# Router logits formed in the attention stage instead of in the experts stage

## The reference

```python
x = x + tanh(g_xattn) * attention(layernorm(x), ctx, mask)      # 4 heads of 128, one key/value head, rope, softmax over 64
z = layernorm(x)                                                # the attention output x1, normed
logits = einsum('bntd,des->bntes', z.reshape(b, 32, 32, 512), Wc) + bc + tie     # 32 experts x 4 sets = 128 columns
perm = (logits == logits.max(axis=-3, keepdims=True))           # in each group of 32 tokens one token a column
picked = einsum('bntd,bntes->bnesd', z, perm)
inner = relu(picked @ W1 + b1)                                  # 32 wide, per expert and set
result = inner @ W2 + b2
x = x + tanh(g_ffn) * einsum('bnesd,bntes->bntd', result, perm)
```

## Time and profile before

| what | value |
|---|---|
| time, median of 3 runs | 1773.8 us (1768.51 to 1779.29) |
| the profiled execution's own time | 1778.45 us |
| its span, first to last instruction | 1776.7 us |
| mean granted TensorE clock | 0.987 of full speed |
| transfers | 325.90 MB, mean 183 GB/s |

### The profile page before, as it was taken

One profiled execution on the slowest core, in us unless ns is written; L12 is line 12 of the kernel. 1 busy time (PEld: TensorE's weight loads), 2 busy tenths in 40 slices (PEclk: granted clock), 3 DMA queues, 4 the chain that ended last, 5 costly groups with the idle time before them and its releaser, 6 DMA issues.

```text
span 1776.7 us, 53886 instructions
## 1 busy us (share of the span) xinstructions
PE 1663.9 (94%) x23384; PEld 1184.5 (67%) x23384; DVE 1335.7 (75%) x1974; ACT 822.0 (46%) x1073; POOL 623.2 (35%) x847
## 2 busy tenths in 40 slices
PE   7899999999999999979999999999999999999985
PEld 4677777777777777776576567657656765765662
DVE  6777777777777777737788778778877877787776
ACT  3433333333333333445555555565555556555542
POOL 3577777777777777410110011011011101100101
PEclk9999999999999999989999999999999999999997
DMA  7345454545555545353675575576457556645754
GB/s 263 130 144 167 144 173 151 178 151 183 159 167 155 168 144 176 120 187 104 227 238 156 197 247 178 184 236 234 155 200 249 177 194 227 241 150 201 247 180 155
DMA packets 161450, 325.90 MB, mean 183 GB/s; under 512 B 17344, under 2 KB 23232, under 8 KB 155840
## 3 DMA queue, kind: packets, MB, share of 16 engines
q1 hardware_dynamic: 156608, 288.91, 49.9%
q10 hardware_dynamic: 4608, 33.56, 4.8%
HBM read 254.25 MB, written 68.16 MB: 181 GB/s over the span
## 4 chain that ended last, share of the span: by engine, by line
PE 57%; DVE 15%; POOL 10%; issue 9%; ACT 5%; DMA 2%; SPq 0%; DVEq 0%; POOLq 0%; ACTq 0%
PE ps L1309 13%; PE ps L1282 8%; PE ps L1336 8%; PE ps L214 6%; PE ps L844 6%; PE ps L1351 4%; POOL qc L486 4%; POOL qc L487 4%; PE ps L200 4%; PE ps L1331 3%; DVE mx L612 2%; DVE qs L629 2%; PE ps L807 2%; DVE qc L628 2%; PE ps L787 2%
## 5 line engine op out<-in xcount | busy, mean ns | idle before, releaser
L182 POOL TENSOR_TENSOR b_va<-b_mv,eps_layer 128x2 f32<-128x2 f32 x64 | 12.5, 196 | 833.6 <-DVE b_mv L173 832.7
L1194 DVE STREAM_TRANSPOSE res<-res 128x2048 f32<-128x2048 f32 x128 | 292.0, 2295 | 0.1
L1146 ACT ACTIVATE gat<-ps 128x1536 f32<-128x1536 f32 (+1 forms) x128 | 172.2, 1345 | 198.2 <-PE ps L1282 198.2
L787 PE MATMUL ps<-xTh,qh 128*128 128x512 f32 x512 | 208.6, 407 | 7.0 <-DVE qs L629 5.4
L787 PE MATMUL ps<-xTl,qh 128*128 128x512 f32 x512 | 200.2, 391 | 0.0
L787 PE MATMUL ps<-xTh,ql 128*128 128x512 f32 x512 | 199.8, 390 | 0.0
L1216 DVE COPY res<-ps 128x1024 f32<-128x1024 f32 x128 | 156.7, 1224 | 43.7 <-PE ps L1336 43.7
L1282 PE MATMUL ps<-sel,xin 32*128 32x128 f32 x4096 | 153.7, 283 | 27.9 <-ACT sel L242 13.5
L1156 ACT ACTIVATE res<-ps 128x1024 f32<-128x1024 f32 x128 | 131.2, 1025 | 92.8 <-PE ps L1336 92.8
L1282 PEld LDWEIGHTS ps<-sel,xin 32*128 32x128 f32 x4096 | 129.4, 186 | 63.0 <-ACT gat L1146 40.1
L475 POOL TENSOR_TENSOR xTl<-xT,xTh 128x512 fp32r<-128x512 f32 x128 | 160.7, 1286 | 10.9 <-ACT xTh L522 10.9
(11 more groups left out here) (132 smaller groups left out, 3217.1 us busy)
## 6 DMA issues: line engine op xcount, KB each, us to landing
xin<-x_scratch SPq DMA_DIRECT2D x196, 256.0 KB, 4.0
xT<-in_xT SPq DMA_DIRECT2D x32, 1024.0 KB, 5.9
xin<-in_x SPq DMA_DIRECT2D x64, 512.0 KB, 3.8
x_scratch<-xin SPq DMA_DIRECT2D x64, 512.0 KB, 3.1
xin<-in_W SPq DMA_DIRECT2D x128, 256.0 KB, 3.5
gat<-in_W ACTq DMA_DIRECT2D x32, 1024.0 KB, 8.5
xT<-in_W SPq DMA_DIRECT2D x68, 256.0 KB, 4.0
gat<-in_W SPq DMA_DIRECT2D x64, 256.0 KB, 3.8
```

The source lines that it names most:

```text
L787: last = e.matmul(ps[:, 2 + n % 2, :], a[:, c, n * DH:(n + 1) * DH], b[:, c, :], start=(k == 0), stop=(k == len(parts) - 1))
L1146: e.activation(o, v, ACT.Copy).then_inc(m_gaA.sem, 1)
L1194: e.transpose(v, v).then_inc(m_tr.sem, 1)
```

## The change

The logits are linear in x1 up to the layer norm's factor and mean, and x1 is x plus probabilities times values times output weights. So the router weights are centred once (their mean over the width is taken off), and the logits before scaling are the sum of two products made in the attention stage: x by the centred weights (`part_of_x`, 12 fp32r matmuls a unit, before the probabilities are transposed), and the probabilities by `values * output weights * centred router weights` (`part_of_values`, 6 fp32r matmuls a unit, before `values`). The weights for the second are made in the set-up. ACT copies the first part, DVE adds the second (`both_parts`), and SP stores the 512 columns of a unit to `lg_scratch`. DVE also takes the statistics of x1 there, POOL makes the layer norm's factors (`row_scale`), and these are stored to `r_scratch`. The experts stage loads logits and factors by halves (`load_logits`), POOL multiplies them (`scaled`) and norms the x tiles (`normed`, formerly ACT), and DVE picks. Both halves use one place in SBUF, so the second load waits for the first pick. `turn`, `across`, `logits`, `stats` and `scale` are gone; the evictions of `outer` are divided 10 to 6 between ACT and DVE, the picks stand between DVE's evictions, the banks of `outer` are swapped, and the second of ACT's W2 loads stands behind the first eviction.

```diff
+W2_BY_ACT = ((0, 0), (1, 0), (2, 0), (2, 1), (3, 0), (4, 0), (5, 0), (5, 1), (6, 0), (7, 0))
+W2_BY_DVE = ((0, 1), (1, 1), (3, 1), (4, 1), (6, 1), (7, 1))
...
+    vc_dram = nc.dram_tensor("vc_scratch", (B, P, 2 * E), F32, kind="Internal").ap()
+    lg_dram = nc.dram_tensor("lg_scratch", (B, 2, E, HT), F32, kind="Internal").ap()
+    r_dram = nc.dram_tensor("r_scratch", (B, 2, P, TH), F32, kind="Internal").ap()
...
-    def stats(self, e, i, k):
-        for t in (2 * k, 2 * k + 1):
-            e.wait_ge(self.d_x[t].sem, self.d_x[t].at(i))
...
-    def scale(self, e, i, k):
...
+    def load_logits(self, e, i, h):
+        if h:
+            e.wait_ge(self.m_eq.sem, self.m_eq.at(i, 0))
+        v = self.room(i)
+        e.dma_start(v[:, 0:HT], self.lg_dram[i, h]).then_inc(self.d_lg.sem, 16)
+        e.dma_start(v[:, HT:2 * HT], self.r_dram[i, h].rearrange("p t -> (p t)").partition_broadcast(P)).then_inc(self.d_lg.sem, 16)
...
     def normed(self, e, i, t):
...
+        e.wait_ge(self.d_x[t].sem, self.d_x[t].at(i))
+        e.wait_ge(self.m_r.sem, self.m_r.at(i, t // TH))
+        e.tensor_scalar(self.xn[:, t, :], self.xn[:, t, :], self.r[:, i, t:t + 1], self.nb[:, i, t:t + 1],
+                        ALU.mult, ALU.add).then_inc(self.m_xn.sem, 1)
...
+    def scaled(self, e, i, h):
+        e.wait_ge(self.d_lg.sem, self.d_lg.at(i, 2 * h + 1))
+        v = self.room(i)
+        o = v[:, 0:HT].rearrange("p (t s) -> p t s", s=P)
+        e.tensor_tensor(o, o, v[:, HT:2 * HT].rearrange("p (s t) -> p t s", t=TH), ALU.mult).then_inc(self.m_lr.sem, 1)
...
+        v = groups(self.room(i)[:, 0:HT])
+        e.wait_ge(self.m_lr.sem, self.m_lr.at(i, h))
...
-        e.wait_ge(self.m_xT.sem, self.m_xT.at(i, 6 + h))
...
+            def store_r(u):
+                e.wait_ge(route.m_r.sem, route.m_r.at(u // 2, u % 2))
+                e.dma_start(route.r_dram[u // 2, u % 2], route.r[:, u // 2, u % 2 * TH:(u % 2 + 1) * TH]).then_inc(d_r.sem, 16)
...
+            e.dma_start(owT, out_wT.rearrange("p (c h) -> p c h", c=C)).then_inc(d_owT.sem, 16)
...
+                if u == NU - 2:
+                    for n in range(2):
+                        e.wait_ge(d_lgs[n].sem, d_lgs[n].at(B - 2))
+                    e.wait_ge(d_r.sem, d_r.at(NU - 4))
+                    e.wait_ge(m_Q.sem, m_Q.at(NU - 1, H - 1))
+                    route.load_logits(e, 0, 0)
+                if u == NU - 1:
+                    route.load_logits(e, 0, 1)
+                e.wait_ge(m_ls.sem, m_ls.at(u))
...
+                    if h and u:
+                        store_r(u - 1)
...
+            def row_scale(u):
+
+                k, i, v = u % 2, u // 2, slice(u % 2 * TH, (u % 2 + 1) * TH)
+                e.wait_ge(m_ag1.sem, m_ag1.at(u))
...
+            def part_of_x(u):
+                e.wait_ge(m_LX.sem, m_LX.at(u))
+                if u >= 2:
+                    e.wait_ge(d_lgs[u % 2].sem, d_lgs[u % 2].at(u // 2 - 1))
+                e.activation(lx[:, u % 2, :], ps[:, 7, :], ACT.Copy).then_inc(m_lx.sem, 1)
...
+            def stats_of_x1(u, t):
+                e.wait_ge(m_rs.sem, m_rs.at(u, t))
+                e.bn_stats(bst1[:, u % 2, t, :], xin[:, u % RING, t, :]).then_inc(m_s1.sem, 1)
...
+            def both_parts(u):
+                e.wait_ge(m_LP.sem, m_LP.at(u))
+                e.tensor_tensor(lx[:, u % 2, :], ps[:, 7, :], lx[:, u % 2, :], ALU.add).then_inc(m_ls.sem, 1)
...
+            def part_of_x(u):
...
+                parts = [(a, b, c) for c in range(C) for a, b in ((wch, xTh), (wch, xTl), (wcl, xTh))]
+                for k, (a, b, c) in enumerate(parts):
+                    last = e.matmul(ps[:, 7, :], a[:, c, :], b[:, c, :], start=(k == 0), stop=(k == len(parts) - 1))
+                last.then_inc(m_LX.sem, 1)
...
+            def part_of_values(u):
...
+                parts = [(a, b, p) for p in range(2) for a, b in ((voh, pTh), (voh, pTl), (vol, pTh))]
+                for k, (a, b, p) in enumerate(parts):
+                    last = e.matmul(ps[:, 7, :].rearrange("p (t c) -> p t c", c=P), a[:, p, :], tiles(b, p), start=(k == 0), stop=(k == len(parts) - 1))
+                last.then_inc(m_LP.sem, 1)
...
+                    for m in range(H):
+                        for c in range(C):
+                            last = e.matmul(ps[:, 2, m * E:(m + 1) * E], owT[:, c, m * DH:(m + 1) * DH], wc[:, c, :],
+                                            start=(c == 0), stop=(c == C - 1), skip_group_check=True)
+                    last.then_inc(m_oc.sem, 1)
+                    e.wait_ge(m_ocl.sem, m_ocl.at(0))
...
+                    for i, (v, w) in enumerate(((vTh, owc[0]), (vTh, owc[1]), (vTl, owc[0]))):
+                        last = e.matmul(ps[:, j % 2, :], v[:, 2 * j * S:(2 * j + 2) * S], w, start=(i == 0), stop=(i == 2))
+                    last.then_inc(m_vcp.sem, 1)
...
+                    part_of_x(g + 1)
...
+                    part_of_values(g)
...
-        bank = lambda u: 4 - u % 2 * 4
+        bank = lambda u: u % 2 * 4
...
-        beside = [[], [], [], [("T", 0)], [("T", 1), ("lg", 0), ("T", 2), ("lg", 1)], [("T", 3), ("lg", 2), ("T", 4), ("lg", 3)],
-                  [("T", 5), ("lg", 4), ("T", 6), ("lg", 5)], [("T", 7), ("lg", 6), ("lg", 7), ("sT", 0)]]
...
+                for what, t in (("x", 0), ("x", 1), ("y", 0), ("y", 1), ("x", 2), ("x", 3), ("y", 2), ("y", 3)):
...
+                if live(i + 1):
+                    e.wait_ge(m_w1.sem, m_w1.at(i, 6))
+                    route.load_logits(e, i + 1, 0)
...
+                if live(i + 1):
+                    for t in range(TH, NT):
+                        load_x(i + 1, t)
+                if live(i - 1) and i < B:
...
+                if live(i + 1):
+                    route.load_logits(e, i + 1, 1)
...
+                for t in range(TH):
+                    route.normed(e, i, t)
+                route.scaled(e, i, 0)
+                for t in range(TH, NT):
+                    route.normed(e, i, t)
+                route.scaled(e, i, 1)
...
+                load_second(e, i, W2_MOVED[0])
+                for u, jp in W2_BY_ACT:
+                    rest(i, u, jp)
+                    if (u, jp) == (0, 0):
+                        load_second(e, i, W2_MOVED[1])
...
+                for u, jp in W2_BY_DVE if live(i) else ():
+                    if live(i + 1) and (u, jp) == W2_BY_DVE[1]:
+                        pick(i + 1, 0)
+                    if live(i + 1) and (u, jp) == W2_BY_DVE[4]:
+                        pick(i + 1, 1)
+                    rest(i, u, jp)
...
-                    if i:
-                        e.wait_ge(m_fin.sem, m_fin.at(i - 1, NT - 1))
-                elif live(i + 1):
...
+                elif i:
+                    e.wait_ge(m_fin.sem, m_fin.at(i - 1, NT - 1))
...
-                    for o, k in beside[t] if live(i + 1) else ():
-                        {"T": turn, "lg": logits, "sT": chosen_T}[o](i + 1, k)
...
+                for h in range(2):
+                    if live(i + 1):
+                        chosen_T(i + 1, h)
```

More of the change, by code:

```diff
@@ L567, in scalar @@
             for g in range(-1, NU):
-                if g == NU - 1:
-                    for t in range(4, 8):
-                        route.normed(e, 0, t)
                 if unit(g):
@@ L861, in tensor @@
             last.then_inc(m_qm.sem, 1)
+            e.wait_ge(d_wc.sem, d_wc.at(0))
+            for c in range(C):
+                last = e.matmul(ps[:, 6, 0:E], mean_of, wc[:, c, :], start=(c == 0), stop=(c == C - 1))
+            last.then_inc(m_wm.sem, 1)
             for h in range(2):
@@ L951, in experts @@
         sb = lambda n, s, dt=F32: st.enter_context(nc.sbuf_tensor(n, s, dt))
-        NV, NY = route.NV, TH
-        wc, bcol, b1r, b2s, rowk, part, tie = consts
-        xn, sel = route.xn, route.sel
+        NY = TH
+        bcol, b1r, b2s, rowk, part, tie = consts
+        xn = route.xn
         gat = sb("gat", [P, 2, E * NG])
+        selT = [sb(f"selT{k}", [P, T]) for k in range(2)]
+        sel = sb("sel", [P, NT, E])
         res = sb("res", [P, Q * D])
@@ L1372, in tensor @@
                             gather(i, n)
-                        if n == 0 and i:
-                            chosen_T(i, 1)
                         if n == 1:
```

426 lines of the change are left out of this document (202 added, 224 removed).

## The result

The changed kernel takes 1897.1 us, the median of four runs (1896.8 to 1899.4), where the kernel before takes 1773.9; the ratio is 1.070, 95% interval 1.066 to 1.073. The profiled execution has a span of 1895.3 us against 1776.7 before, with a mean granted clock of 0.944 where it was 0.987.

The account below looks back on a forecast made before the run. PE was taken to bound attention; in the experts PE gets time back and transfers show next. Attention plus 129 and experts minus 88 made plus 41 on 1778.45, 1820, or 1815 for the median; range 1765 to 1852 us.

Parts of the forecast that it names:

- rival D: Attention: POOL or DVE late by 1 us a unit, plus 32 us, 1847 us; chance 0.17.
- the step on the last W2 piece: Experts: 7.86 MB at 390 GB/s, start and landing must pass before `outer(7)`, which starts at S+24.0.
- S: Experts: the start of the scatter in a batch, from which the forecast lays out its times in us.
- outer(1) at S+9.3: Experts: `outer(1)` waits for DVE's last finish of the y tiles, put at S+9.2.
- The way out: Experts, `outer(7)` to next gather: 1.6 plus 2.4 us through DVE's last evictions, gather at S+28.0.
- DVE picks until S+24.9: Experts: second logits land at S+21, POOL multiplies, DVE picks, then evicts 6 and 7 until S+27.4.
- Rival E: Experts: changed W2 order makes the second piece late for `outer(6)`, PE's clock falls; period 60, 1857 us; chance 0.03.
- Rival B: Experts: transfers don't matter, `outer(7)` at S+21.2, period 53.9 to 54.2, result 1770 to 1776 us; chance 0.14.

Follow-up runs that it names:

- part_third: The changed kernel with `part_of_x` cut from 12 matmuls to 4 a unit, leaving out the two correction products; 1837 us.
- x_early: The changed kernel with SP issuing x tiles 4 and 5 ahead of the logits and y 4 to 7; 1856 us.
- y_first: x_early, with x 4 and 5 waiting for no other x and ACT's first W2 piece issued only once y 4 to 7 landed; x_early's time.
- no_logits: The changed kernel without loads of logits and row scales and POOL's product for batches 1 to 15; minus 18 us.
- neither: The changed kernel without logits, row scales and product in batches 1 to 15, and without the last W2 piece's load; minus 113 us.
- thin: The changed kernel with y stores, last W2 quarters and loads of logits and row scales cut to a quarter of their columns, order kept; 1815 us.
- w2_less: The changed kernel without the load of the last W2 piece, `outer(7)` multiplying with the piece before; minus 2 us.

## Why the prediction was wrong

The direction was right, the time was not: 1897 us lies above the forecast 1815 and above the range, which ended at 1852.

**Attention: right.** Plus 129 was forecast up to the first gather, 130.9 was measured. The period of a unit is 24.98 (25.1 forecast), the first query starts at 63.63 (65), DVE and POOL follow, so rival D did not occur. `part_third` gives 1.69 us a unit back of the 1.82 that it takes from PE, so PE is what pays.

**Experts: wrong, minus 88 forecast, minus 12.3 measured.** The scatter takes 7.08 as said. The period is 61.9, not 57.0, and 14 x 4.9 = 69 of the missing 76 us are in it; batch 0 takes 58.6 us instead of 53.8, and from the scatter in batch 15 to the end it takes 53.4, some 2 more than forecast. By the prediction's own steps:

- *"at 390 that is 20.2 us, plus 1.5 to start and 2.3 for the last quarter's own wait and landing"*, in the step on the last W2 piece, is the term that failed: S+24.0 forecast, S+28.0 measured. Its bytes and its rate were both off. From S to `outer(7)` the queues moved 8.80 MB, not 7.86. The first logits, issued 2 us before S, and the W1 pieces, issued behind the last quarter, were not counted. The whole burst ran at a mean of 315 GB/s where the step amounts to 328. Less the 3.8 us of start and landing it is 8.80 MB in 24.2 us, or 364 GB/s. So of the 4.0 us missing, 2.4 are 0.94 MB at 390 and 1.6 the lower rate.
- The idea behind the term, one rate that turns bytes into time, did not hold either. These are means over the same 14 batches, from S to the start of `outer(7)`:

```
kernel       outer(7)   MB moved   GB/s   busy share of the queues
after            28.0       8.80    315   0.91
x_early          25.6       8.59    336   0.95
y_first          24.3       8.62    355   0.97
no_logits        26.9       7.86    293   0.84
neither          21.0       6.45    307   0.87
thin             21.2       5.40    255   0.76
```

- The first three move nearly the same bytes, and their order alone gives 315, 336 or 355 GB/s. `no_logits` moves just the 7.86 MB of the forecast and still starts `outer(7)` at S+26.9, because its quarters wait for stores to land. The chain shown with the profile after says the same: 4.54 us for a stored tile to land and 5.23 for the quarter behind it, where the step had 2.3 us for the last quarter's wait and landing beyond its share of the bytes. The earlier trace rows had 3.9 us for such a quarter with nothing beside it. Bytes count too: `thin`, with 3.4 MB less in the burst, gets to S+21.2, with about 1 us of waiting for W2 left.
- I took 386 and 416 GB/s from two windows of 5 us because their share was near 1, as if a busy queue had one rate. The kernel before shows otherwise, in its window just ahead of the one in the earlier trace rows:

```profile
1230.00:1235.00 5.00, 5.00 (x45) 3.82 (x42) 3.33 (x11) 3.63 (x6) 2.56 (x8) 1.00 1.03 311
```

- Stores were issued in or shortly before all three windows, so their presence alone does not tell them apart. The Trainium skill's figure ("DMA: Bandwidth & Descriptors", section "Where 436 GB/s comes from", some 358 GB/s on the HBM side), weighed in the prediction, pointed the right way. The traces do not show it as a bound: the mean of the burst, 315, lay below it, and one burst of `y_first` moved 376 GB/s over 22.6 us. The measurement decides.
- *"outer(1) at S+9.3"*: measured 10.9. The prediction's own terms give 9.6 and not 9.2 for the last finish (12.3 less 2.7). The y tiles took 8.7 us to land in the batch shown, and `y_first`, which keeps a W2 piece out of their way, has `outer(1)` at S+8.8. In the kernel after this costs nothing by itself, since `outer(7)` waits anyway.
- *The way out*, 4.0 us forecast, took 4.66. PE idles for several us ahead of `outer(7)`, and behind it the granted clock was 0.60 (of the two levels, 1.2 GHz for part and 2.4 for the rest). I had left this to the range. The gather stage took 29.3, not 28.9.
- *"DVE picks until S+24.9"*: in the batch shown it picks until S+28.5 (1252.31). The chain hangs on the same queue and slipped with it, so that `w2_less` gained nothing. That both would slip together was in no rival.

Rival E came nearest (period 60, 1857), for another reason and with a chance of 0.03, and it is still 40 us short. Rival B's period, 54, is what `neither` shows when both waits are gone; at 54.5 and with 2 MiB less to move it is 1785 us. So B's step was sound, but its condition needs less traffic than the kernel has. (B's experts should read minus 127 to 131: 14 x 8.05 + 14.4 is 127.)

**What stays open.** How much of the burst's low rate is due to SP's waits for x 4 and for stored tiles, to stores beside loads, to the 256 KB broadcast of row scales or to the number of transfers in flight was not separated. That no order of these bytes would do better than a period of 58.6 is not shown, only that six others did not.

## What to carry to other kernels

Taking work off the engine that bounds a loop gives time back only as far as the transfers that this work had covered: lay the loop out from the moment its burst of transfers starts, and price that burst by the mean of a whole burst, its start, its landings and what is still in flight at its start included, not by its best window. Follow the chain of landings too: a load into the place of a stored tile pays for both. Two waits on one queue can slip together; here removing either alone gave 18 and 2 us of 113, so remove both before concluding that neither matters. Before moving a transfer earlier, ask whose landing it will share the queue with.

## What the runs showed that was not expected

- Nearly the same share of busy queues, 0.94 to 1.03, went with rates from 294 to 416 GB/s in windows of 5 us. Over whole bursts nearly the same bytes moved at 315, 336 or 355 GB/s, by their order alone.
- An earlier issue can cost time: moving x 4 and 5 ahead gained 41 us in the full kernel and lost 22 us in the thinned one. In the full one the wait for W2 shrank and the wait for the y tiles took its place.
- After 3.46 us of idleness PE ran the last `outer` and the turn of `selT` in 1.79 and 1.94 us; with the gap filled by matmuls, in 1.14 and 1.09, at a granted clock of 1.00.
